# Query and key projections on half arrays: two row groups, two banks, and who adds the partial sums

## What is computed

```python
q = to_heads(hidden_states @ Wq, DK)
k = to_heads(hidden_states @ Wk, DK)
v = to_heads(hidden_states @ Wv, DV)
s = jnp.clip(to_heads(hidden_states @ Ws, M), CLAMP_MIN, CLAMP_MAX)
# z = cumlogsumexp(s) over tokens; g = exp(z_before - z); p = exp(s - z)
# hk = hk * g + k p^T;  okT = q hk;  pv = softmax(okT)
# hv = hv * g + p v^T;  ov = pv hv
o = o * rsqrt(mean(o * o) + EPS) * g_norm_weight * silu(hidden_states @ Wg)
return o.reshape(b, t, VALUE_DIM) @ Wo
```

## Time and profile before

| | us |
|---|---|
| median of 3 runs | 1370.15 |
| lowest and highest | 1368.17, 1373.04 |
| the profiled execution | 1372.1 |
| its span in the trace | 1370.4 |
| PE busy in the span | 1334.8 (97%) |
| DVE busy | 810.3 (59%) |
| ACT busy | 459.9 (34%) |
| POOL busy | 255.0 (19%) |

### The profile page before, as it was taken

The page is one execution under the profiler, slowest core; times in us unless marked ns, Lnnn a source line. Parts: engine busy times, 40 slices in busy tenths (PEclk is TensorE's granted clock), DMA queues, the critical chain, the costliest instruction groups (busy, mean ns, idle before and its releaser), DMA issues. The chain is left out here.

```text
span 1370.4 us, 21875 instructions
## 1 busy us (share of the span) xinstructions
PE 1334.8 (97%) x8224; PEld 1149.7 (84%) x8224; DVE 810.3 (59%) x1554; ACT 459.9 (34%) x1370; POOL 255.0 (19%) x238
## 2 busy tenths in 40 slices
PE   7999999999999999999999999999999999899998
PEld 6788888888888888888888888888888888778886
DVE  5556655566665556566655556666555656745544
ACT  5333333343333433343234333333333323511210
POOL 3111411122112301231114111221122111300000
PEclk9999999999999999999999999999999999999999
DMA  6000200001000100010001000010000210000000
GB/s 199 16 1 1 55 1 17 1 23 32 17 1 24 32 17 1 6 49 17 1 1 47 8 18 0 24 32 17 1 24 23 62 32 1 1 2 31 32 31 31
DMA packets 35309, 31.87 MB, mean 23 GB/s; under 512 B 7568, under 2 KB 28048, under 8 KB 35216
## 3 DMA queue, kind: packets, MB, share of 16 engines
q1 hardware_dynamic: 35216, 30.44, 7.6%
HBM read 26.24 MB, written 4.19 MB: 22 GB/s over the span
## 5 line engine op out<-in xcount | busy, mean ns | idle before, releaser
L850 PE MATMUL p<-wvg_hi,xt_hi 128*128 128x512 f32 x512 | 211.6, 413 | 0.1
L852 PE MATMUL p<-wvg_hi,xt_lo 128*128 128x512 f32 x512 | 202.1, 395 | 0.0
L851 PE MATMUL p<-wvg_lo,xt_hi 128*128 128x512 f32 x512 | 201.5, 394 | 0.0
L494 ACT ACTIVATE v_tok<-p 128x256 f32<-128x256 f32 x128 | 49.6, 387 | 345.2 <-PE p L852 345.2
L655 DVE SCALAR_TENSOR_TENSOR gate<-th,p 128x256 f32<-128x256 f32 x128 | 53.9, 421 | 180.0 <-ACT th L498 177.3
L850 PE MATMUL p<-xt_hi,wsqk_hi 128*128 128x512 f32 x384 | 150.1, 391 | 1.4 <-DVE xt_lo L794 1.4
L851 PE MATMUL p<-xt_lo,wsqk_hi 128*128 128x512 f32 x384 | 149.8, 390 | 0.0
L852 PE MATMUL p<-xt_hi,wsqk_lo 128*128 128x512 f32 x384 | 149.4, 389 | 0.0
L438 POOL TENSOR_TENSOR orstd<-ovar,minus_half 128x8 f32<-128x8 f32 x32 | 52.4, 1638 | 453.0 <-DVE ovar L777 453.0
L432 POOL TENSOR_TENSOR v_lo<-v_tok,v_hi 128x256 fp32r<-128x256 f32 x96 | 83.9, 889 | 195.7 <-ACT v_hi L503 195.7
L852 PEld LDWEIGHTS p<-wvg_hi,xt_lo 128*128 128x128 f32 x512 | 97.1, 190 | 22.7
(11 more groups left out here) (191 smaller groups left out, 2796.1 us busy)
## 6 DMA issues: line engine op xcount, KB each, us to landing
acc<-in_L_attn_hidden_states SPq DMA_DIRECT2D x4, 1024.0 KB, 7.5
raw<-in_L_attn_Wv SPq DMA_DIRECT2D x32, 128.0 KB, 2.3
raw<-in_L_attn_Wg SPq DMA_DIRECT2D x32, 128.0 KB, 2.8
raw<-in_L_attn_Wo SPq DMA_DIRECT2D x16, 256.0 KB, 3.2
out<-acc SPq DMA_DIRECT2D x16, 256.0 KB, 2.3
raw<-in_L_attn_Ws SPq DMA_DIRECT2D x8, 256.0 KB, 2.7
raw<-in_L_attn_Wq SPq DMA_DIRECT2D x8, 256.0 KB, 2.8
raw<-in_L_attn_Wk SPq DMA_DIRECT2D x8, 256.0 KB, 3.0
```

The source lines that it names most:

```text
L494: nc.scalar.activation(v_tok[:, c, :], PB[bk][:, 0:VW], ACT.Copy).then_inc(v_done, 1)
L850: nc.tensor.matmul(out_, lh, rh, start=(k == 0), stop=False)
L851: nc.tensor.matmul(out_, lh, rl, start=False, stop=False)
L852: last = nc.tensor.matmul(out_, ll, rh, start=False, stop=(k == n - 1))
```

## The change

Queries and keys of the next cell are no longer made by `feature_proj` but by a new function, `halves_proj`. Each of the 12 matmuls becomes two: one with rows 0 to 63 of both operands, one with rows 64 to 127, so that each uses one half of the array's rows. The upper halves add up in one bank and the lower halves in another, and the projection is the sum of the two banks. The query's two banks are SB[0] and SB[1]; the key's are the two PB banks, as two uses `k0` and `k1`. ACT copies the first bank (the query's scaled), and DVE adds the second to it: `queries_vector` and `keys_vector`. The first cell still uses `feature_proj`. The reciprocal is cut in three: columns 0 to 255, then 256 to 383, then 384 to 511, with the new additions between the pieces and the third piece behind the masked scores. PE waits for `q_done` before `head_blocks(SB, ...)`, because the query's sums lie in the banks SB.

```diff
-P_USES = ["vg0", "vg1", "wo0", "wo1", "wo2", "wo3", "vg2", "vg3", "s", "q", "k", "a0", "a1"]
-AHEAD = ("s", "q", "k", "a0", "a1")
+P_USES = ["vg0", "vg1", "wo0", "wo1", "wo2", "wo3", "vg2", "vg3", "s", "k0", "k1", "a0", "a1"]
+AHEAD = ("s", "k0", "k1", "a0", "a1")
...
         def queries_scalar(act, m):
-            bk, _ = p_turn(m.shifted(-1), "q")
-            ps = PB[bk]
             act.wait_ge(q_proj, m.count(1, 1))
-            scale = float(DK) ** -0.5
-            nc.scalar.activation(q_t[:], ps[:], ACT.Copy, scale=scale).then_inc(q_done, 1)
+            if first(m):
+                ps = PB[p_turn(m.shifted(-1), "k0")[0]]
+                nc.scalar.activation(q_t[:], ps[:], ACT.Copy, scale=Q_SCALE).then_inc(q_done, 1)
+            else:
+                nc.scalar.activation(q_t[:], SB[0][:], ACT.Copy, scale=Q_SCALE).then_inc(q_upper, 1)
 
         def keys_scalar(act, m):
-            bk, _ = p_turn(m.shifted(-1), "k")
+            bk, _ = p_turn(m.shifted(-1), "k1" if first(m) else "k0")
             act.wait_ge(k_proj, m.count(1, 1))
-            nc.scalar.activation(k_t[:], PB[bk][:], ACT.Copy).then_inc(k_done, 1)
+            nc.scalar.activation(k_t[:], PB[bk][:], ACT.Copy).then_inc(k_done if first(m) else k_upper, 1)
...
-        def inverse_vector(dve, m):
-            dve.wait_ge(z_done, m.count(1, 1))
-            nc.vector.reciprocal(rz_t[:], rz_t[:]).then_inc(rz_done, 1)
+        def inverse_vector(dve, m, part):
+            if part == 0:
+                dve.wait_ge(z_done, m.count(1, 1))
+            cols = (slice(0, 2 * P), slice(2 * P, 3 * P), slice(3 * P, 4 * P))[part]
+            nc.vector.reciprocal(rz_t[:, cols], rz_t[:, cols]).then_inc(rz_done, 1)
+
+        def queries_vector(dve, m):
+
+            dve.wait_ge(q_upper, m.count(1, 0))
+            nc.vector.scalar_tensor_tensor(out=q_t[:], in0=SB[1][:], scalar=Q_SCALE, in1=q_t[:], op0=ALU.mult,
+                                           op1=ALU.add).then_inc(q_done, 1)
+
+        def keys_vector(dve, m):
+            bk, _ = p_turn(m.shifted(-1), "k1")
+            dve.wait_ge(k_upper, m.count(1, 0))
+            nc.vector.tensor_tensor(k_t[:], PB[bk][:], k_t[:], ALU.add).then_inc(k_done, 1)
...
                 sums_vector(dve, nxt)
-                inverse_vector(dve, nxt)
+                inverse_vector(dve, nxt, 0)
+                queries_vector(dve, nxt)
+                inverse_vector(dve, nxt, 1)
+                keys_vector(dve, nxt)
...
                 scores_kept(dve, nxt, 0)
                 scores_kept(dve, nxt, 1)
+                inverse_vector(dve, nxt, 2)
...
+        def halves_proj(pe, m, i, done):
+
+            if i == 1:
+                banks = SB
+            else:
+                uses = [p_turn(m.shifted(-1), use) for use in ("k0", "k1")]
+                banks = [PB[bk] for bk, _ in uses]
+                for _, before in uses:
+                    wait_read(pe, p_read, before)
+            if m.j is not None and m.b == B:
+
+                pe.wait_ge(w_lo_done, (m.j + 1) * 7 + (i + 1))
+            b = m.batch
+            for kt in range(KT):
+                for n, (w_part, x_part) in enumerate(((wsqk_hi, xt_hi[b]), (wsqk_hi, xt_lo[b]), (wsqk_lo, xt_hi[b]))):
+                    for half in range(2):
+                        rows_own = slice(half * DK, (half + 1) * DK)
+                        mm = nc.tensor.matmul(banks[half][:], w_part[rows_own, i, kt, :], x_part[rows_own, kt, :],
+                                              start=(kt == 0 and n == 0), stop=(kt == KT - 1 and n == 2))
+            mm.then_inc(done, 1)
...
-            pe.wait_ge(rz_done, cell.count(1, 1))
+            pe.wait_ge(rz_done, cell.count(3, 3))
...
                 feature_proj(pe, nxt, 0, s_proj)
-                feature_proj(pe, nxt, 1, q_proj)
-                feature_proj(pe, nxt, 2, k_proj)
+                halves_proj(pe, nxt, 1, q_proj)
+                halves_proj(pe, nxt, 2, k_proj)
...
             pe.wait_ge(pz_t_done, cell.count(1, 1))
             pe.wait_ge(k_tok_done, cell.count(1, 1))
+            if not last:
+                pe.wait_ge(q_done, nxt.count(1, 1))
             head_blocks(SB, e, pz_t, weights)
```

More of the change, by code:

```diff
@@ L305, in attention @@
         weights, values, rows = sem("weights"), sem("values"), sem("rows")
+        q_upper, k_upper = sem("q_upper"), sem("k_upper")
         s_clipped, e_done, z_done, rz_done = sem("s_clipped"), sem("e_done"), sem("z_done"), sem("rz_done")
@@ L365, in attention @@
         X1 = [SB[1], SB[0], XB, OB]
+        Q_SCALE = float(DK) ** -0.5
         def first(cell):
@@ L806, in _ @@
             scores_kept(dve, m, 1)
-            inverse_vector(dve, m)
+            for part_ in range(3):
+                inverse_vector(dve, m, part_)
             dve.wait_ge(gn_half, 1)
@@ L828, in _ @@
                 add_rows(dve, tail, c)
-        p_read = {"s": (s_clipped, 1, 2), "q": (q_done, 1, 2), "k": (k_done, 1, 2),
+        p_read = {"s": (s_clipped, 1, 2), "k0": (k_done, 1, 2), "k1": (k_done, 1, 2),
                   "a0": (scores_masked, 2, 3), "a1": (scores_masked, 2, 4)}
@@ L855, in feature_proj @@
         def feature_proj(pe, m, i, done):
-            bk, before = p_turn(m.shifted(-1), "sqk"[i])
+            bk, before = p_turn(m.shifted(-1), ("s", "k0", "k1")[i])
             wait_read(pe, p_read, before)
```

## The result

The changed kernel runs in 1410.9 us (median of 4; 1408.7 to 1416.7) against 1369.2 for the kernel before in the same comparison: a ratio of **1.0304, 95% interval 1.0271 to 1.0338**, some 42 us slower. The forecast was 1378.2, in a range up to 1386. The direction was right; the size was off by a factor of five.

The account below looks back on a forecast made before the run. PE bounds each cell, with DVE's masks nearly late; 31 cells at 0.26 us make 8.1 us, more loop instructions 0, so 1378.2 us against a median of 1370.15. Range 1370.5 to 1386 us.

Parts of the forecast that it names:

- the slack of DVE: Between DVE's masks and PE's values: 0.17 us, about 0.1 us of it spare after the semaphore.
- The pairs at 226.5 ns: In the q and k projections: two halves side by side cost one full matmul, 226.5 ns a pair, no gain.
- (a): Rival for q and k: pairs stream faster than full matmuls, at 220 ns, +4.0 us, 1374.2 us; chance 24%.
- (b): Rival for q and k: pairs are dearer, 234 ns, 13.3 us more, 1383.5 us; chance 15%.
- (c): Rival for q and k: fp32r halves of 512 columns take turns, 169 us more, 1539 us; chance 5%.
- the hint from the float32 pairs: At L1006: float32 pairs take 110 ns, full-array matmuls of that kind about 112, so halves run side by side.
- the range's lower end of 1370.5: Whole kernel: the range's lower bound, the floor of rival (a), pairs streaming faster than full matmuls.
- The switch, 0.19 us, moved and not added: Full array to halves on PE: moves from behind keys to ahead of queries; q and k land 0.19 us later.
- The chain to the masks, 0.26 us a cell: Keys' last pair, ACT's copy, DVE's addition, masks: values start at 573.98 instead of 573.72, 0.26 us later a cell.
- The sign that I had named: In the changed trace: PE idle before the values, some 0.25 us in each of 31 cells, formerly no entry.
- The sum's line on "more instructions in the loop": PE's loop boundaries: 9% more matmuls might add 1.0 us to the 11.2 us of idle time; taken as 0.
- The chance of "slower": Whole kernel slower by over 0.3%: 70%, from 50% for the forecast, 15% for (b), 5% for (c).

Follow-up runs that it names:

- u_adds_only: Kernel before with PE's loop written out, full matmuls kept, DVE's additions (the same bank once more) and reciprocal pieces put in: 1360.5 us, ratio 0.9933.
- before_pad48: Kernel before, still looped, with 24 identity transposes (48 instructions) at PE's start: 1398.4 us, ratio 1.0183.
- before_pad24: Kernel before, still looped, with 12 identity transposes (24 instructions) at PE's start: 1372.6 us, ratio 1.001.

## Why the prediction was wrong

- **What bounds the kernel, and the slack of DVE:** right in kind. DVE is idle ahead of the masks once the additions are gone. The slack was smaller than 0.1 us: in `u_adds_only`, as in the changed kernel, PE starts the values 0.146 us behind the end of the masks, and in the kernel before it was 0.175. So 0.03 was spare; about as much again comes back between the first and the second matmul of the values (0.18 us instead of 0.21), and a little more later in the cell.
- **The pairs at 226.5 ns:** right. From the start of one pair to the next the trace has 227 for the keys' and 224 to 236 for the queries' behind the switch; the 23 steps take 5.37 us where 5.31 were forecast. Rivals (a), (b) and (c) are all out; the hint from the float32 pairs held for fp32r. Of the rivals' figures, 220 ns was twice the 110 ns of a float32 pair and 234 ns was 226.5 and 7 for the distance between the halves' starts, both my estimates; no run shows the 213 ns a pair that stand behind the range's lower end of 1370.5, and the runs showed 224 to 236. With nothing won in the pairs there was nothing to lose on DVE for.
- **The switch, 0.19 us, moved and not added:** right (0.32 and 0.33 for two steps), and the keys landed 0.25 us later where I had 0.20.
- **The chain to the masks, 0.26 us a cell:** the values started 0.37 to 0.38 later, and a cell grew by 0.30 to 0.33. The addition began at 6.33 behind the clip (6.28 forecast); the rest is the step from DVE's end to PE's start, 0.14 us and not the 0.06 that I took from one row. Part of this error was given back, as said above, so that 31 cells made 10 us, not 8: the figure is nearer than the working deserves. The sign that I had named, PE idle before the values in the list of waits, did not appear; the wait is there, under the matmuls' listed time.
- **The sum's line on "more instructions in the loop", 0 to 1.0 us, taken as 0: this is the step that failed.** It was 33 us. I scaled the 11.2 us of pauses with the number of instructions, as if they were a share of work. They are an event per return, whose price hung on how many instructions lay between the loop's first and the end of its 256-instruction block: six second pauses, 16.7 and 18.5 us in all, with about 15 (`before_pad48` and the changed kernel), none with about 40 or more. The 49 instructions that the change added *ahead* of the loop took that from about 64 to about 15. The pauses have `issue` as their releaser, in six places, all at the loop's start; that alone should have made me ask what supplies PE with instructions at a return before I priced them. And with a pause of 3 us behind one of 2 us the granted clock was 0.50 for 6.8 us at every return (for 3.4 us at two of six before; 0.983 as the mean of the span, where it was 0.995), which a count of idle time leaves out: of the 5.4 us more at each return some 3.1 are the pause (18.5 / 6) and, by my estimate, most of the rest is the slower clock: 5.2 of the 6.8 us lie behind the restart in the return shown, at half speed, which makes 2.6.
- The chance of "slower" was 70%, for the reason given; most of the loss came by a road that no rival named. The range missed it, and would have held the kernel had its loop begun elsewhere: with 64 instructions in front the same change ran in 1381.4.

## What to carry to other kernels

PE's loop had a price at each return that depended on where its first instruction fell in the instruction blocks: the cell with the return was 6.4 to 8.6 us longer than the others with about 15 instructions left, 1.8 to 3.8 with about 40 or more (the other engines' loops were not tested); so a change that adds instructions anywhere ahead of such a loop must be compared at several places, or with the loop written out, before its own worth is read from the time. Where "issue" ends an idle stretch at a loop's start, try the written-out loop first: here it was worth 1.1%, and the change of the arithmetic lost time. Two halves of the array side by side cost here what one full matmul costs (0.03 us a cell more), so with a contraction that is already 128 long they brought nothing, and each switch between full and half cost 0.2 us of PE.

## What I had not expected of the hardware

- The second pause was longer than the first: 2.4 to 3.7 us against 1.5 to 2.2. The next block's transfer started 0.7 to 2.2 us after PE had restarted, whether PE had 15 instructions left or 200, and a stalled PE went on 1.2 to 1.6 us after it had ended. Behind the first block it was the same: PE restarted 1.5 to 1.7 us after the end of its transfer.
- About 40 instructions left (with twelve long matmuls among them) hid that just so (no second pause in `before_pad24`), about 15 didn't (pauses of 2.4 to 3.7 us). What lies between wasn't tried.
- The first pause (1.5 to 2.2 us) stayed in every looped kernel, with a body of 1928 instructions as with 2120; ten blocks were fetched in a pass of either (eleven in one).
- After both pauses of the changed kernel the granted clock was 0.50 at the start of the next cell, 0.63 as a mean of the 6.8 us from 369.6 to 376.4 in the return shown; in the kernel before a cell with a return was 37.8 to 38.3 us long where the clock stayed at 1.00, and 39.8 to 39.9 where it was 0.50 for 3.4 us.
